# Sorting the rows of three batches by expert instead of two, in a one-core attention and mixture-of-experts kernel

## The chip, the cores and the metric

The kernel runs on one core of one Trainium2 chip. The metric is the time in microseconds (us) of one execution on the device.

## What is computed

Four batches of 512 tokens, each a row of 256 float32. Cut to its shape, the reference is:

```python
h = W_tok[x]                                                     # 4 x 512 x 256
h = h + local_attention(layernorm(h)) @ Wo + bo                  # 16 heads, windows of 128, one window back
n = layernorm(h)
gate = softmax(n @ W_gate + b_gate)                              # 8 experts
combine = top-2 weights of gate, zero elsewhere                  # 4 x 512 x 8
moe = sum over e of combine[e] * (n @ W_experts[e] + b_experts[e])
out = h + full_attention(n @ W_qkv + b_qkv) + moe
```

Each row needs only two of the eight experts.

## The kernel before

The program is written engine by engine with semaphores between them. The attention runs in eight **stages**, in the order of `STAGES` (line 55): LOCAL 0, LOCAL 1, LOCAL 2, FULL 0, LOCAL 3, FULL 1, FULL 2, FULL 3, numbered 0 to 7. A stage has 16 **slots** (a group of four heads and a block of 128 keys each), and a slot has two **half slots**, so a stage has half slots t = 0 to 31. In a slot TensorE computes transposed scores (`scores`, lines 1478 and 1484), row scores of a later head (`row_scores`, lines 1456 to 1464), of which VectorE takes the maxima (`maxima`, line 971 in a FULL stage) through two PSUM banks `SC`, and probabilities times V (`times_v`, line 1505). ScalarE takes the exponentials (lines 840 and 843). The last stage has no rows of a later stage, so its slots 10 to 15 have no row scores and no maxima.

All else is laid into the half slots by the table `PREPS` (line 60): an entry `(what, batch, first)` of stage s starts the work `what` of that batch at half slot `first` of that stage; entries with a negative `first` continue from the stage before. `prep_jobs` (line 210) says at which step which job of TensorE comes; each engine and the DMA queues run the same table. All jobs of TensorE outside the slots go through two PSUM banks `R` in turn (`claim`, line 1229: a job waits until the job two before it has been read). The kinds that matter here:

- `"full"`: layer norm, transposes into `xT_full`, q, k, v, gate logits and the choice of two experts (`gate_weights`, line 1034) of a batch's FULL stage. `"out"`: the projection after local attention.
- `"dense"`, for batches 2 and 3: every expert takes all 512 rows. 16 jobs `dx` (line 1377), one in two half slots, each two row tiles of 128 by one expert; VectorE multiplies by the weight and adds it into `h` (line 1133).
- `"route"`, `"experts"`, `"combine"`, for batches 0 and 1 (`SPARSE = 2`): the rows are sorted by expert. `count_rows` (line 1337) and the steps of lines 1073 to 1105 find each row's place. GpSimd scatters the normalised rows into `x_sorted` in DRAM (`sort_rows`, line 650, 16 indirect DMAs, one a half slot). With 16 row tiles of pairs and up to 8 tiles that are filled in part there are 24 tiles, each of one expert. A job `xs` transposes two tiles (line 1359), loaded by SyncE (line 553); a job `ex` multiplies them by their experts' weights (line 1373), gathered by GpSimd (line 666, 256 KB each); VectorE copies the result (line 1119), SyncE stores it (line 559). `combine` gathers each row's two results (line 682) and VectorE adds them into `h` (line 1147).

SyncE and GpSimd run their DMAs in program order; a wait holds whatever is behind it. On SyncE these are the q/k parts (line 491), the stacked loads for the next stage (line 505), the shift rows (line 512), the loads and stores of sorted tiles, expert weights of dense batches (line 570) and the output (line 523). Before the scatters, SyncE zeroes `x_sorted` in stage 3 (line 545).

Of the kernel before, what the change touches and what calls it, by code (L numbers as in the profile page):

```python
# [82 lines left out]
SPARSE = 2  # L83
# [179 lines left out]
def tower(nc, x, tok_w, wq, bq, wk, bk, wv, bv, wo, bo, wqkv, bqkv, wg, bg, wexp, bexp, out):  # L263
    with ExitStack() as ctx:
# [200 lines left out]
        def _(sp):  # L465
# [96 lines left out]
            def load_weights(b, e):  # L562

                n = W_BEFORE[b] + e
                if n == 0:
                    sp.wait_ge(s_qk_ps, at(STAGE[LOCAL, B - 1], 4, 4))
                    sp.wait_ge(s_v_ps, V_BEFORE[STAGE[LOCAL, B - 1] + 1])
                if n >= W_RING:
                    sp.wait_ge(s_ex_ps, last_bank(n - W_RING) + 1)
# [12 lines left out]
            for s in range(len(STAGES)):  # L582
                kind, b = STAGES[s]
                for u in range(UNITS):
# [25 lines left out]
        def _(pool):  # L610
# [49 lines left out]
            def gather_weights(j):  # L660
# [11 lines left out]
            def gather_output(n, k):  # L672
                if n == 0 and k == 0:
# [101 lines left out]
        def _(act):  # L775
# [12 lines left out]
            def copy_x(p, c):  # L788
# [777 lines left out]
```

## Time and profile before

| | us |
|---|---|
| median of 3 runs | 643.25 (642.73 to 643.69) |
| the profiled execution | 642.01 |
| its span, first to last instruction | 640.2 |
| busy: TensorE / VectorE / ScalarE / GpSimd | 561.2 / 419.1 / 296.3 / 182.7 |
| mean granted TensorE clock | 0.959 of full speed |

The profile shows one execution. Stages are told apart by their first transposed-score matmul: stage 3 begins at 225.33 us of the span, stage 4 at 295.87, stage 5 at 362.42, stage 6 at 461.61, stage 7 at 556.00. A float32 matmul stands as two records in the trace. An engine's busy share is an average over these stages.

### The profile page before, as it was taken

To read this page: it belongs to the slowest core of one execution; us is meant where nothing else is said; L and a number is where in the kernel's file an instruction comes from. 1 tells how busy PE (TensorE), PEld (TensorE's weight loads), DVE (VectorE), ACT (ScalarE), POOL (GpSimd) and SP (SyncE) were. 2 spreads that over 40 slices of the span, in tenths; PEclk is the share of its full clock that TensorE was granted. 3 is DMA by queue.
4 is the path that set the end of the run, shared out by engine and by line. 5 is a ranking of instruction groups with operands and counts; after the bars stand their busy time and mean duration, and the time that the engine had idled before them with its cause. 6 is when DMAs were issued, how large, how long until landed. Compare 5 with 4: busy or idle time off the path is not lost.

```text
span 640.2 us, 9968 instructions
## 1 busy us (share of the span) xinstructions
PE 561.2 (88%) x3455; PEld 301.9 (47%) x3455; DVE 419.1 (65%) x940; ACT 296.3 (46%) x558; POOL 182.7 (29%) x238
## 2 busy tenths in 40 slices
PE   3867699889999898998998899989998898999994
PEld 3434455555565333444543455544444454555441
DVE  7237557675867888577478777756865465678830
ACT  0312346444644575476264353535554454444452
POOL 3774216222322501022132233211143231043201
PEclk9879799999989999999797799999999899999998
DMA  6386425342344235532325134504149668232310
GB/s 171 106 171 135 128 59 173 64 94 62 109 84 83 83 104 129 132 104 79 83 49 167 43 84 124 124 9 132 50 143 253 181 171 225 68 93 73 100 51 33
DMA packets 42417, 69.23 MB, mean 108 GB/s; under 512 B 6648, under 2 KB 35968, under 8 KB 39296
## 3 DMA queue, kind: packets, MB, share of 16 engines
q1 hardware_dynamic: 38144, 56.02, 34.4%
q0 software_dynamic: 4224, 12.59, 6.7%
q8 instruction: 28, 0.46, 0.3%
q14 instruction: 21, 0.17, 0.1%
HBM read 45.25 MB, written 23.07 MB: 107 GB/s over the span
## 4 chain that ended last, share of the span: by engine, by line
PE 66%; DVE 16%; issue 6%; DMA 6%; ACT 2%; SPq 2%; POOL 1%; POOLq 0%; DVEq 0%; ACTq 0%
PE OB L1505 11%; PE R L1387 9%; PE R L1285 8%; PE SC L1456 7%; PE ST L1478 6%; PE R L1300 5%; DVE neg_max L971 4%; PE SC L1461 3%; PE R L1373 3%; DMA QS<-shiftT 2%; PE ST L1484 2%; DMA xs<-x_sorted 2%; PE R L1333 2%; PE R L1402 2%; PE SC L1464 2%
## 5 line engine op out<-in xcount | busy, mean ns | idle before, releaser
L971 DVE TENSOR_REDUCE neg_max<-SC 128x1 f32<-128x512 f32 x256 | 171.1, 686 | 93.2 <-PE SC L1456 89.2
L840 ACT ACTIVATE prob<-ST 128x512 f32<-128x512 f32 x256 | 136.8, 598 | 125.1 <-PE ST L1478 119.2
L1505 PE MATMUL OB<-prob,VS 128*32 128x512 f32 (+2 forms) x1024 | 108.3, 496 | 0.1
L1456 PE MATMUL SC<-KS,QS 96*128 96x512 bf16 x256 | 98.1, 392 | 8.7 <-DVE neg_max L971 6.5
L843 ACT ACTIVATE prob<-ST 128x512 f32<-128x512 f32 (+1 forms) x128 | 68.5, 544 | 79.8 <-PE ST L1484 79.1
L709 POOL TENSOR_SCALAR_AFFINE_SELECT prob<-prob 128x512 f32<-128x512 f32 x64 | 41.0, 640 | 154.4 <-ACT prob L843 154.3
L1478 PE MATMUL ST<-QS,KS 98*128 98x512 bf16 x256 | 78.6, 384 | 2.0 <-ACT prob L840 1.9
L979 DVE TENSOR_REDUCE neg_max<-SC 128x2 f32<-128x512 f32 x64 | 44.1, 688 | 25.7 <-PE SC L1464 25.4
L976 DVE TENSOR_REDUCE neg_max<-SC 128x1 f32<-128x128 f32 (+1 forms) x128 | 39.4, 349 | 30.1 <-PE SC L1464 30.0
L1461 PE MATMUL SC<-KS,QS 96*128 96x256 bf16 (+1 forms) x256 | 55.3, 269 | 3.8 <-DVE neg_max L976 1.9
L1484 PE MATMUL ST<-QS,KS 98*128 98x256 bf16 (+1 forms) x256 | 48.1, 271 | 9.4 <-DMA QS<-shiftT 9.4
L1464 PE MATMUL SC<-mask_q,ident_bf 128*128 128x128 bf16 x256 | 51.6, 225 | 0.0
L781 ACT ACTIVATE parts<-R,qk_bias 128x512 bf16<-128x512 f32 x32 | 22.0, 687 | 60.0 <-PE R L1285 58.4
L1456 PEld LDWEIGHTS SC<-KS,QS 96*128 96x128 bf16 x256 | 25.0, 98 | 51.2 <-DVE neg_max L971 32.8
L695 POOL TENSOR_TENSOR parts<-rest,parts 128x512 bf16<-128x512 f32 x32 | 37.3, 1168 | 40.1 <-ACT parts L786 22.4
L944 DVE SCALAR_TENSOR_TENSOR rest<-R,qk_bias,parts 128x512 f32<-128x512 f32 x32 | 23.9, 748 | 27.3 <-ACT parts L781 26.3
L719 POOL TENSOR_TENSOR h<-h,AO 128x256 f32<-128x256 f32 x16 | 11.6, 727 | 102.3 <-DVE AO L1013 74.6
L1478 PEld LDWEIGHTS ST<-QS,KS 98*128 98x128 bf16 x256 | 24.7, 98 | 32.2 <-ACT prob L840 11.2
L1461 PEld LDWEIGHTS SC<-KS,QS 96*128 96x128 bf16 x256 | 25.3, 101 | 27.9 <-DVE neg_max L976 10.2
L1505 PEld LDWEIGHTS OB<-prob,VS 128*32 128x32 f32 x1024 | 20.4, 109 | 36.7 <-issue 33.1
L1285 PE MATMUL R<-xT_full,w_qkv 128*128 128x512 f32 x64 | 33.0, 608 | 3.0 <-DVE VS L956 3.0
L1484 PEld LDWEIGHTS ST<-QS,KS 98*128 98x128 bf16 x256 | 22.7, 102 | 25.3 <-issue 17.2
(147 smaller groups left out, 807.2 us busy)
## 6 DMA issues: line engine op xcount, KB each, us to landing
scratch<-parts SPq DMA_DIRECT2D x96, 128.0 KB
QS<-scratch SPq DMA_DIRECT2D x16, 384.0 KB, 5.2
KS<-scratch SPq DMA_DIRECT2D x16, 384.0 KB, 4.9
QS<-scratch SPq DMA_DIRECT2D x16, 256.0 KB, 3.8
KS<-scratch SPq DMA_DIRECT2D x16, 256.0 KB, 4.5
x_sorted<-ys SPq DMA_DIRECT2D x24, 128.0 KB, 3.5
xs<-x_sorted SPq DMA_DIRECT2D x12, 256.0 KB
y_sorted<-ys SPq DMA_DIRECT2D x12, 256.0 KB
```

Source lines behind the costliest of these rows:

```text
L840: act.activation(prob[:, u % 2, e, :], src[:, :], ACT.Exp, scale=SCALE).then_inc(s_prob, 1)
L843: act.activation(prob_local[:, u % 2, u // 2 % 2, 2 * e:2 * e + 2, 0:w], src[:, :].rearrange("p (i w) -> p i w", i=2)[:, :, 0:w], ACT.Exp, ...
L971: dve.tensor_reduce(own_max[:, i, head:head + 1], bank[:, :], AX.X, ALU.max, negate=True).then_inc(s_max, 1)
L979: dve.tensor_reduce(own_max[:, 2:4, head], bank[:, :].rearrange("p (w k) -> p w k", w=2), AX.X, ALU.max, negate=True).then_inc(s_max, 1)
L1285: mm = pe.matmul(bank[:, :], w, xT_of(p)[:, c, :], start=(c == 0), stop=(c == NC - 1))
L1387: mm = pe.matmul(bank[:, t % 2 * D:(t % 2 + 1) * D], xT_full[b % 2][:, c, t * P:(t + 1) * P], w_exp[n % W_RING][:, c, :], start=(c == 0), ...
L1456: pe.matmul(bank[:, :], Q[0:SHIFT_ROW, head, i * P:(i + 1) * P], K[0:SHIFT_ROW, head, :], start=True, stop=True).then_inc(s_sc_ps, 1)
L1461: pe.matmul(bank[:, first:last], Q[0:SHIFT_ROW, head, w * P:(w + 1) * P], K[0:SHIFT_ROW, head, max(w - 1, 0) * P:(w + 1) * P], start=(w % ...
L1464: mm = pe.matmul(bank[:, last - P:last], ident_bf[:, :], mask_q[:, :], start=False, stop=(w % 2 == 1), skip_group_check=True)
L1478: mm = pe.matmul(bank[:, :], K[0:KROWS, g * GH + e, keys], Q[0:KROWS, g * GH + e, :], start=True, stop=True)
L1484: mm = pe.matmul(bank[:, i * 2 * P:i * 2 * P + w], K[0:KROWS, head, keys], Q[0:KROWS, head, kt * P:kt * P + w], start=(i == 0), stop=(i == 1),
L1505: mm = pe.matmul(OB[VW * i:VW * (i + 1), columns], VS[s % 3][:, kt, v:v + VW], p_of, start=(kt == 0), stop=(kt == NT - 1), skip_group_chec ...
```

## The change

Batch 2 is sorted as well: `SPARSE` is 3, so there are 24 scatters (two a half slot), 32 expert tiles and 16 jobs `xs` and `ex`; only batch 3 stays dense. `PREPS` is laid out anew, the rings of expert weights and of results get a sixth and a third buffer, `xT_full` has one buffer instead of two, and batch 3's normalised rows go into batch 0's buffer once its rows are scattered.

```diff
     3: (("out", 2, 0), ("full", 1, 9)),
-    4: (("full", 1, -23), ("full", 2, 1), ("route", 0, 28), ("dense", 2, 32)),
-    5: (("route", 0, -4), ("dense", 2, 0), ("out", 3, 0), ("full", 3, 9), ("experts", 0, 36)),
-    6: (("full", 3, -23), ("experts", 0, 4), ("dense", 3, 29)),
-    7: (("experts", 0, -28), ("dense", 3, -3), ("combine", 0, 2), ("combine", 1, 10)),
+    4: (("full", 1, -23), ("full", 2, 1), ("route", 0, 24), ("experts", 0, 56)),
+    5: (("route", 0, -8), ("out", 3, 0), ("full", 3, 9), ("experts", 0, 24)),
+    6: (("full", 3, -23), ("experts", 0, -8), ("dense", 3, 25), ("combine", 0, 29)),
+    7: (("dense", 3, -7), ("combine", 0, -3), ("combine", 1, 5), ("combine", 2, 13)),
...
-SPARSE = 2
+SPARSE = 3
...
-BLOCKS = 2 * NT * 2
+BLOCKS = PAIR_TILES
...
-SCATTER_STEP = 4
+SCATTER_STEP, SCATTERS = 4, 2
 DENSE_JOBS = 2 * E
-W_RING, X_RING, Y_RING = 5, 3, 2
+W_RING, X_RING, Y_RING = 6, 3, 3
...
-        xT_full = [sb(f"xT_full{k}", [P, NC, T]) for k in (0, 1)]
+        xT_full = sb("xT_full", [P, NC, T])
...
-            return xn_local if kind == LOCAL or b >= SPARSE else xn_full[b]
+            return xn_local if kind == LOCAL or b == 2 else xn_full[b % 3]
...
-                    for b, slot in ((2, 3), (0, 8), (1, 12)):
+                    for b, slot in ((0, 6), (1, 10), (2, 14)):
...
                     for n in range(PAIR_TILES * TOP_K):
-                        if step == SCATTER_STEP + n:
+                        if step == SCATTER_STEP + n // SCATTERS:
                             sort_rows(n)
...
-                if kind == FULL and b > 1:
-                    act.wait_ge(s_qk_ps, at(STAGE[FULL, b - 2], 4, 4))
-                    act.wait_ge(s_v_ps, V_BEFORE[STAGE[FULL, b - 2] + 1])
+                if kind == FULL and b > 0:
+                    act.wait_ge(s_qk_ps, at(STAGE[FULL, b - 1], 4, 4))
+                    act.wait_ge(s_v_ps, V_BEFORE[STAGE[FULL, b - 1] + 1])
...
+                    if (kind, b) == (FULL, 3):
+                        dve.wait_ge(s_sorted[0], 16 * NT * TOP_K)
```

How the jobs of TensorE lie in the half slots before and now, as the table gives them:

| | before | now |
|---|---|---|
| stage 4 | `route` at t = 28 | `route` at t = 24 |
| stage 5 | 16 `dx` of batch 2, t = 0 to 30 | 4 `xs`, 3 `ex`, t = 24 to 30 |
| stage 6 | 12 `xs`, 12 `ex`, t = 4 to 28; 2 `dx` | 12 `xs`, 13 `ex`, t = 0 to 24; 4 `dx` |
| stage 7 | 14 `dx`, t = 1 to 27 | 12 `dx`, t = 1 to 23 |

TensorE in slots 0 and 1 of stage 5 (`w_q` holds an expert's weights there); before:

```order
L1478 MATMUL ST<-QS,KS 128x512 x2
L1456 MATMUL SC<-KS,QS 128x512
L1505 MATMUL OB<-prob,VS 32x128 x4
L1456 MATMUL SC<-KS,QS 128x512
L1478 MATMUL ST<-QS,KS 128x512 x2
L1456 MATMUL SC<-KS,QS 128x512
L1323 MATMUL R<-ident,AO 128x128 x4
L1387 MATMUL R<-w_q,xT_full 128x256 x2
L1456 MATMUL SC<-KS,QS 128x512
L1387 MATMUL R<-w_q,xT_full 128x256 x2
L1478 MATMUL ST<-QS,KS 128x512 x2
L1456 MATMUL SC<-KS,QS 128x512
```

and now:

```order
L1477 MATMUL ST<-QS,KS 128x512 x2
L1455 MATMUL SC<-KS,QS 128x512
L1504 MATMUL OB<-prob,VS 32x128 x4
L1455 MATMUL SC<-KS,QS 128x512
L1477 MATMUL ST<-QS,KS 128x512 x2
L1455 MATMUL SC<-KS,QS 128x512
L1322 MATMUL R<-ident,AO 128x128 x4
L1455 MATMUL SC<-KS,QS 128x512
L1477 MATMUL ST<-QS,KS 128x512 x2
L1455 MATMUL SC<-KS,QS 128x512
```

The matmuls of batch 2's dense expert are gone from between the attention's; the rest stands in the same order.

SyncE at the end of stage 5 (`parts` are batch 3's q and k); before:

```order
L505 DMA KS<-scratch 32x1x4096
L505 DMA QS<-scratch 16x4096
L570 DMA w_v<-in_L_ffn_W_experts 128x2x256
L491 DMA scratch<-parts 8x16x512 x6
L505 DMA KS<-scratch 16x4096
L512 DMA QS<-shiftT 1x4x512 x2
L491 DMA scratch<-parts 8x16x512 x6
L553 DMA xs<-x_sorted 128x2x256 x2
L512 DMA QS<-shiftT 1x4x512 x2
L505 DMA QS<-scratch 48x1x4096
L553 DMA xs<-x_sorted 128x2x256
L505 DMA KS<-scratch 48x4096
```

and now:

```order
L510 DMA QS<-shiftT 1x4x512 x2
L503 DMA QS<-scratch 32x1x4096
L551 DMA xs<-x_sorted 128x2x256
L503 DMA KS<-scratch 32x1x4096
L551 DMA xs<-x_sorted 128x2x256
L503 DMA QS<-scratch 16x4096
L489 DMA scratch<-parts 8x16x512 x6
L551 DMA xs<-x_sorted 128x2x256
L503 DMA KS<-scratch 16x4096
L551 DMA xs<-x_sorted 128x2x256
L510 DMA QS<-shiftT 1x4x512 x2
L489 DMA scratch<-parts 8x16x512 x6
```

Four loads of sorted tiles (line 551 now) moved ahead, between the stacked loads and the writes of the parts; the stage's last pair of shift rows, which had none ahead of it, now has four.

GpSimd from stage 4's end through stage 5; before:

```order
L709 AFFINE_SELECT prob<-prob 128x4x128 x6
L656 DMA x_sorted<-xn_full,slots 3072x256 x11
L689 TENSOR_TENSOR var_eps<-var,eps 128x4
L691 TENSOR_TENSOR rstd<-var_eps,minus_half 128x4
L656 DMA x_sorted<-xn_full,slots 3072x256
L719 TENSOR_TENSOR h<-h,AO 128x4x64
L656 DMA x_sorted<-xn_full,slots 3072x256 x4
L719 TENSOR_TENSOR h<-h,AO 128x4x64
L695 TENSOR_TENSOR parts<-rest,parts 128x512 x4
L719 TENSOR_TENSOR h<-h,AO 128x4x64
L666 DMA w_exp<-in_L_ffn_W_experts,w_rows 128x512 x2
```

and now:

```order
L706 AFFINE_SELECT prob<-prob 128x4x128 x5
L650 DMA x_sorted<-xn_full,slots 4096x256 x4
L706 AFFINE_SELECT prob<-prob 128x4x128
L650 DMA x_sorted<-xn_full,slots 4096x256 x12
L650 DMA x_sorted<-xn_local,slots 4096x256 x8
L686 TENSOR_TENSOR var_eps<-var,eps 128x4
L688 TENSOR_TENSOR rstd<-var_eps,minus_half 128x4
L716 TENSOR_TENSOR h<-h,AO 128x4x64 x2
L692 TENSOR_TENSOR parts<-rest,parts 128x512
L663 DMA w_q<-in_L_ffn_W_experts,w_rows 128x512
L663 DMA w_k<-in_L_ffn_W_experts,w_rows 128x512
L692 TENSOR_TENSOR parts<-rest,parts 128x512
```

All 24 scatters now stand ahead of batch 3's layer norm, with one mask of local probabilities between the fourth and the fifth, and gathers of weights stand between batch 3's third parts.

## Rows read from the trace of the kernel before

**Rows 1.** The page, part 4: shares of the chain that ended last:

```profile
PE 66%; DVE 16%; issue 6%; DMA 6%; ACT 2%; SPq 2%; POOL 1%; POOLq 0%; DVEq 0%; ACTq 0%
```

**Rows 2.** Windows, stages 3 to 7: length, PE, PEld, DVE, ACT, POOL busy, clock, DMA, GB/s:

```profile
225.33:295.87 70.54, 65.98 (x392) 29.38 (x389) 51.96 (x121) 44.92 (x86) 8.13 (x9) 1.00 0.43 113
295.87:362.42 66.55, 57.19 (x391) 28.99 (x390) 47.03 (x117) 27.95 (x53) 16.66 (x23) 0.87 0.34 92
362.42:461.61 99.19, 95.11 (x488) 52.12 (x485) 70.77 (x156) 45.68 (x86) 23.67 (x25) 0.98 0.32 81
461.61:556.00 94.39, 84.03 (x457) 45.59 (x456) 56.34 (x97) 45.76 (x85) 25.71 (x28) 0.98 0.65 182
556.00:640.25 84.25, 72.90 (x385) 35.51 (x383) 48.75 (x103) 37.70 (x72) 18.76 (x21) 0.97 0.21 66
```

**Rows 3.** The page, part 5: the maxima of a FULL stage:

```profile
L971 DVE TENSOR_REDUCE neg_max<-SC 128x1 f32<-128x512 f32 x256 | 171.1, 686 | 93.2 <-PE SC L1456 89.2
```

**Rows 4.** TensorE in order of time, stage 5: start, us, instructions, idle before:

```profile
397.39 1.13 PE L1387 MATMUL R<-w_exp,xT_full 128*128 128x256 f32 x4
398.36 0.38 PE L1456 MATMUL SC<-KS,QS 96*128 96x512 bf16 x1
398.57 1.03 PE L1387 MATMUL R<-w_exp,xT_full 128*128 128x256 f32 x4
399.44 0.60 PE L1478 MATMUL ST<-QS,KS 98*128 98x512 bf16 x2
```

**Rows 5.** TensorE in order of time, stage 6:

```profile
475.94 0.63 PE L1359 MATMUL R<-ident,xs 128*128 128x128 f32 x4
476.40 1.03 PE L1373 MATMUL R<-w_exp,xsT 128*128 128x256 f32 x4
477.27 0.38 PE L1456 MATMUL SC<-KS,QS 96*128 96x512 bf16 x1
477.49 1.03 PE L1373 MATMUL R<-w_exp,xsT 128*128 128x256 f32 x4
478.35 0.60 PE L1478 MATMUL ST<-QS,KS 98*128 98x512 bf16 x2
```

**Rows 6.** Windows, stages 3 and 5: slots 0 to 9, and 10 to 15 of stage 5:

```profile
225.33:271.08 45.75, 42.47 (x237) 18.96 (x234) 33.56 (x71) 26.49 (x50) 1.95 (x3) 1.00 0.50 127
...
362.42:424.62 62.20, 60.58 (x317) 34.67 (x314) 43.25 (x96) 26.93 (x50) 17.57 (x19) 0.98 0.37 90
424.62:461.61 36.99, 34.52 (x172) 17.45 (x171) 27.52 (x60) 18.75 (x36) 6.10 (x6) 1.00 0.24 66
```

**Rows 7.** Windows, single slots: stage 6 slots 0 and 3, stage 7 slots 12 and 13 together, 14:

```profile
461.61:464.76 3.15, 3.02 (x18) 0.78 (x17) 2.54 (x4) 2.75 (x6) 0.58 (x1) 1.00 0.73 216
475.28:480.32 5.04, 5.04 (x30) 2.85 (x28) 3.15 (x5) 3.10 (x6) 0.94 (x1) 1.00 0.62 153
...
615.58:624.95 9.37, 8.73 (x47) 4.64 (x46) 2.43 (x6) 4.72 (x9) 0.00 (x0) 1.00 0.08 27
624.95:627.40 2.45, 2.13 (x14) 0.45 (x12) 0.88 (x2) 1.97 (x4) 1.20 (x2) 1.00 0.01 3
```

**Rows 8.** Waits in stage 6: who waited for whom, us in total, times, longest:

```profile
PE R L1359 <- DMA xs<-x_sorted: 6.1, 3, 2.4
...
DVE ys L1119 <- DMA y_sorted<-ys: 2.9, 2, 1.6
...
PE R L1373 <- DVE AO L1013: 2.6, 2, 1.3
```

**Rows 9.** L656, the scatters: durations ns min/median/max, starts:

```profile
L656 POOL DMA_INDIRECT x_sorted<-xn_full,slots x16: 954/959/1117, 363.9 to 405.0; - x16
```

**Rows 10.** L666, the gathers of expert weights: issue to landing:

```profile
DMA to landing us min/median/max: 3.7/4.0/7.1
```

**Rows 11.** Windows, stage 5 slot 0:

```profile
362.42:367.82 5.40, 5.40 (x29) 3.12 (x25) 3.43 (x9) 2.00 (x4) 1.78 (x2) 0.72 0.07 26
```

**Rows 12.** All in order of time, the last instruction of the engines:

```profile
633.33 0.72 POOL L719 TENSOR_TENSOR h<-h,AO 128x256 f32<-128x256 f32 x1 [4.24 <-DVE AO L1013]
```

More of the change, by code:

```diff
@@ L86 @@
 TILE_JOBS = EXPERT_TILES // 2
-BLOCKS = 2 * NT * 2
+BLOCKS = PAIR_TILES
 ROUTE_STEPS = 13
-SCATTER_STEP = 4
+SCATTER_STEP, SCATTERS = 4, 2
 DENSE_JOBS = 2 * E
-W_RING, X_RING, Y_RING = 5, 3, 2
+W_RING, X_RING, Y_RING = 6, 3, 3
 LOAD_STEP, W_STEP, DENSE_W_STEP, STORE_STEP, ADD_STEP = -4, -3, -4, 4, 6
-EX_BEFORE = {2: 0, 0: DENSE_JOBS, 3: DENSE_JOBS + TILE_JOBS}
-W_BEFORE = {2: 0, 0: E, 3: E + EXPERT_TILES}
+EX_BEFORE = {0: 0, 3: TILE_JOBS}
+W_BEFORE = {0: 0, 3: EXPERT_TILES}
 def at(b, per_batch, k):
@@ L148, in last_bank @@
 def last_bank(n):
-    if n < W_BEFORE[0]:
-        return 2 * n + 1
     if n < W_BEFORE[3]:
@@ L449, in xT_of @@
             kind, b = STAGES[p]
-            return xT_local if kind == LOCAL else xT_full[b % 2]
+            return xT_local if kind == LOCAL else xT_full
         def xn_of(p):
             kind, b = STAGES[p]
-            return xn_local if kind == LOCAL or b >= SPARSE else xn_full[b]
+            return xn_local if kind == LOCAL or b == 2 else xn_full[b % 3]
         def dense_no(b, e):
@@ L564, in load_weights @@
                 n = W_BEFORE[b] + e
[L565 to L569, printed above, removed]
+                sp.wait_ge(s_ex_ps, last_bank(n - W_RING) + 1)
                 sp.dma_start(w_exp[n % W_RING][:, :, :], wexp[e].rearrange("(c p) n -> p c n", p=P))\
@@ L604, in _ @@
                 sp.wait_ge(s_written[m], 32 * PARTS * len(STAGES))
-            for k in range(Y_RING):
-                sp.wait_ge(s_stored[k], ring_count(TILE_JOBS - Y_RING + k, Y_RING))
+            for i in range(TILE_JOBS - Y_RING, TILE_JOBS):
+                sp.wait_ge(s_stored[i % Y_RING], ring_count(i, Y_RING))
             sp.wait_ge(s_out, 16 * B)
@@ L664, in gather_weights @@
                     pool.wait_ge(s_route, 13)
-                pool.wait_ge(s_ex_ps, last_bank(n - W_RING) + 1)
+                    pool.wait_ge(s_qk_ps, at(STAGE[LOCAL, B - 1], 4, 4))
+                    pool.wait_ge(s_v_ps, V_BEFORE[STAGE[LOCAL, B - 1] + 1])
+                if n >= W_RING:
+                    pool.wait_ge(s_ex_ps, last_bank(n - W_RING) + 1)
                 pool.indirect_dma_start(
@@ L677, in gather_output @@
                     pool.wait_ge(s_xs_ps, TILE_JOBS)
-                    for j in range(Y_RING):
-                        pool.wait_ge(s_stored[j], ring_count(TILE_JOBS - Y_RING + j, Y_RING))
+                    for i in range(TILE_JOBS - Y_RING, TILE_JOBS):
+                        pool.wait_ge(s_stored[i % Y_RING], ring_count(i, Y_RING))
                 if n >= len(y) and k == 0:
@@ L1386, in dense_expert @@
                     for c in range(NC):
-                        mm = pe.matmul(bank[:, t % 2 * D:(t % 2 + 1) * D], xT_full[b % 2][:, c, t * P:(t + 1) * P],
+                        mm = pe.matmul(bank[:, t % 2 * D:(t % 2 + 1) * D], xT_full[:, c, t * P:(t + 1) * P],
                                        w_exp[n % W_RING][:, c, :], start=(c == 0), stop=(c == NC - 1))
```

## The prediction

> **What bounds the kernel now.** I read the chain of waits first, then busy time by stage, then the order of TensorE's instructions, and last what it waits for. Two thirds of the chain that ended last is TensorE, 16% VectorE [rows 1]. By stage [rows 2], TensorE is busy 95.1 of 99.19 us in stage 5, 84.0 of 94.39 in stage 6 and 72.9 of 84.25 in stage 7; VectorE 70.8, 56.3 and 48.8. So in the stages that the change touches, time that TensorE is spared is time of the kernel, until VectorE's maxima take over. The best measure of that point is stage 3: it is the same FULL attention with the same `out` and `full` work at the same half slots as stage 5, only without dense jobs, and it took 70.54 us against 99.19.
>
> **Prices.** A job `dx` takes, from its start to the next instruction, 0.97 us for its first tile and 0.87 for its second: 1.84 us [rows 4]. A job `xs` takes 0.46 us, a job `ex` 0.87 and 0.86: 1.73 us, together 2.19 [rows 5].
>
> **The change part by part, by TensorE's work.**
> - Stage 5 loses 16 `dx` (-29.4 us) and gains 4 `xs` and 3 `ex` (+1.8 and +5.2): -22.4.
> - Stage 6 gains one `ex` and two `dx`: +1.7 and +3.7 = +5.4.
> - Stage 7 loses two `dx`: -3.7.
> - The count of rows takes four more matmuls of a few columns, under 0.2 us; it comes four half slots earlier in stage 4, where TensorE idles 9 of 66.55 us [rows 2]. VectorE's choice for batch 2 adds five small instructions there. I take 0 for both, with 1 us either way.
>
> Sum: -20.7 us, within one.
>
> **The same by slots, which holds waits too.** Stage 5, slots 0 to 9, took 62.20 us with ten `dx`; the same slots of stage 3 took 45.75 [rows 6]. A FULL slot 0 with no job took 3.15 [rows 7], some 0.6 more than stage 3's, which follows a LOCAL stage; so about 46.3 now, -15.9, or 1.6 a job rather than 1.84, since part of the cover of VectorE's maxima goes. Slots 10 to 15 (36.99 us [rows 6]) lose six `dx` at 1.84 and gain 4 `xs` and 3 `ex`, -11.0 + 7.0 = -4.0. Stage 5 thus takes about 79.3, -19.9. In stage 6 a slot without a job took 3.15 us and one with `xs` and `ex` 5.04 [rows 7]: +1.9 for the pair. Its first slots fill, its last ones change `ex` for `dx`, and one of three waits for a tile's load, which come where the load was queued behind the shift rows (half slots 8, 16, 24), goes, since half slot 24 has no `xs`; another may come at the end of stage 5. The three cost 6.1 us [rows 8]. So +5.4 less about 2, +1 for the new one: +4. In stage 7 slots 12 and 13 take 9.37 us with two `dx`, and slot 14, with none, 2.45 [rows 7]; allowing 0.6 for turning one group of outputs, -3.9. Sum: -19.8. The two ways give -20.7 and -19.8; I take -20.3.
>
> **What is hidden.** Eight more scatters on GpSimd at 0.96 us [rows 9]: all 24 are issued from half slot 28 of stage 4 to 7 of stage 5, four of them ahead of the last mask of local probabilities. That is 24 x 0.96 = 23 us in 12 half slots of about 2 us, so GpSimd may fall a few us behind, and has slot 4 free before batch 3's layer norm needs it in slot 5. The first load of sorted tiles, at half slot 20, waits at the head of SyncE's queue for all of them, with stacked loads, parts and the next shift rows behind it; by then 12 half slots, over 25 us, have passed. Eight more weight gathers, issued four half slots ahead of use, land 4.0 us later at the median, 7.1 at most [rows 10]; the cover is two slots of 5 us, and TensorE waits for none before. Eight more 128 KB zero stores lie in stage 3's slots 12 to 15. Copies on ScalarE and VectorE replace adds, and VectorE's total falls. Four loads and stores more, and eight weight loads fewer, keep SyncE level. Batch 2's output now waits for its gathered rows, but from about half slot 26, two slots before the last store is issued; what stands after the last add (it starts at 633.33 [rows 12]) I leave as it is.
>
> **Sum and forecast.** The profiled execution took 642.01 us, 1.24 under the median. 642.0 - 20.3 = 621.7; against the median of 643.25, **623.0 us**, -3.1%. A difference under 0.2% could not be told from none.
>
> **Rivals.**
> - *VectorE paces the cleared slots.* With two `SC` banks a slot cannot be shorter than four maxima, 4 x 0.686 = 2.7 us [rows 3], plus hand-overs. If the twelve cleared slots of stage 5 gave back half of 20.3, the time would be 633. Against it: stage 3, with VectorE busy 52.0 of 70.54 us and the same work. For it: stage 3's last slots have cheaper rows, stage 5's do not. 0.08.
> - *TensorE's clock.* Less work may lower it. The granted clock was 1.00 in stage 3 without any `dx`, 0.87 in stage 4, which has the idle time, and 0.72 in stage 5's slot 0 [rows 2, 11], the lower level (1.2 GHz) for over half of it. If stage 5's cleared 46 us ran at stage 4's 0.87, 12 us of it would be at 1.2 GHz and up to 6 us longer: 629. The Trainium skill (TensorE: Matmul & The Clock Gate, Part 4: PE-mode transpose) says that transposes do not count as TensorE being busy; by that rule, with 16 more transposes and 52 fewer matmuls in stage 5, this rival would be the forecast, 629. Here stage 6, with the twelve `xs`, was granted 0.98 [rows 2], so the trace does not bear it out. 0.10.
> - *Deeper rings give more.* The third result buffer takes away VectorE's wait for stores (2.9 us), and shifted loads all three waits for tiles (6.1) [rows 8]; if all of both stood on the path, 642.0 - 20.3 - 7 = 614.7, or 616 against the median. 0.06.
> - *Slower: weights arrive late.* Each of 16 `ex` needs two gathered tiles of 256 KB, which now share the DMA engines with batch 3's parts and stage 6's stacked loads at the end of stage 5, where stage 6 alone had a share of 0.65 [rows 2]. It decides from a landing of 10 us on: each us beyond costs 16 us over the sixteen jobs. At 11.5 us it takes 24 and gives 647. The longest landing was 7.1 [rows 10], and none was waited for. 0.03.
> - *The change does not do what it says*, since the freed time only turns into waits, for maxima or banks `R`: about 643. 0.02. Nothing in stage 3 looks like it.
>
> **How the numbers follow.** The forecast has 0.71. Its own range is 619.5 to 626: the two sums, 1 us for stage 4, and up to 3 us for one more stretch at the lower clock. The clock rival (629) is taken in, and half of the first one's give-back: **618.0 to 629.5**. Outside lie most of VectorE's case, late weights, no effect and most of the deeper rings. Faster by over 0.2%: all but the last two, 0.95; within 0.2%: 0.02; slower: 0.03.
>
> **What would show it.** Right: stage 5 about 79 us, stage 6 about 98, stage 7 about 80, stages 0 to 4 as before; 128 fewer records of `dx` matmuls (two for each of 64), and 32 more of `ex`; VectorE's idle time before its maxima smaller in stage 5; TensorE's idle time before `xs` near 6 us. Wrong: stage 5 at 85 or more with TensorE idle before row scores (VectorE), or a clock under 0.9 there (clock); waits of TensorE before `ex` for weights; a wait of `out` or of the end for gathered rows.

## The result and the profile after

| | us |
|---|---|
| the kernel before, median of 4 runs | 643.47 (642.73 to 647.74) |
| the changed kernel, median of 4 runs | 660.09 (655.81 to 663.16) |
| ratio | 1.024, 95% interval 1.0161 to 1.0318 |
| its profiled execution | 662.04, span 660.3 |

In these runs the change made the kernel 2.4% slower; 3.1% faster was forecast. On the page of the changed kernel TensorE is busy for 559.3 us, hardly less than before (561.2), at a lower mean clock (0.926 against 0.959):

```profile
span 660.3 us, 9830 instructions
...
PE 559.3 (85%) x3379; PEld 293.5 (44%) x3379; DVE 415.3 (63%) x925; ACT 298.4 (45%) x562; POOL 207.2 (31%) x262
```

Busy time by stage of the changed kernel, stages 3 to 7 (start and end; length; busy time and count by engine; granted clock, share of the DMA engines, GB/s), against [rows 2]:

```profile
227.30:297.86 70.56, 65.99 (x392) 29.38 (x389) 51.98 (x121) 44.91 (x86) 8.13 (x9) 1.00 0.46 120
297.86:368.71 70.85, 61.13 (x395) 30.54 (x394) 50.62 (x127) 28.13 (x53) 22.15 (x29) 0.80 0.33 95
368.71:466.83 98.12, 80.91 (x401) 36.52 (x397) 58.78 (x121) 47.40 (x90) 36.71 (x39) 0.92 0.40 108
466.83:576.42 109.59, 92.85 (x481) 52.47 (x480) 58.80 (x102) 45.56 (x85) 25.69 (x28) 0.94 0.59 167
576.42:660.31 83.89, 69.43 (x369) 32.54 (x367) 50.27 (x107) 37.60 (x72) 24.68 (x26) 0.96 0.24 71
```

Stage 3 is untouched. In stage 5 TensorE's busy time fell from 95.1 to 80.9 us and VectorE's from 70.8 to 58.8, and yet the stage lasts 98.12 us, as before (99.19). Stage 6 took 15.2 us more, for 5.4 of added work by the prediction's prices (TensorE was busy 8.8 us more in it, at a clock of 0.94 against 0.98). Stage 7's TensorE time fell by 3.5 us as the prediction's step had it, its length by 0.4. What TensorE was spared has turned into waits.

Two kinds of wait are new. The table of waits of the changed kernel (engine, line and what it waited for; us in total, times, longest), four of its rows:

```profile
PE R L1358 <- DMA xs<-x_sorted: 15.3, 4, 6.4
DVE neg_max L970 <- remote: 10.2, 3, 3.7
ACT xT_local L804 <- remote: 6.7, 2, 4.1
POOL x_sorted L650 <- remote: 4.5, 2, 2.4
```

The first was 6.1 in three waits [rows 8]. "Remote" means that the semaphore moved on just before the engine did, but that no instruction which could have moved it ended within 1.5 us before. The kernel before has no such row among its largest waits. The timeline of the changed kernel in stage 5's slot 1 (start, us, engine, line, instruction, idle time before it) shows what it is:

```profile
371.79 0.39 PE L1455 MATMUL SC<-KS,QS 96*128 96x512 bf16 x1
...
372.45 0.38 PE L1455 MATMUL SC<-KS,QS 96*128 96x512 bf16 x1
...
373.31 0.96 POOL L650 DMA_INDIRECT x_sorted<-xn_full,slots  x1 [0.30 <-issue]
374.58 0.96 POOL L650 DMA_INDIRECT x_sorted<-xn_full,slots  x1 [0.31 <-issue]
375.77 0.59 ACT L823 COPY OT<-OB 128x512 f32<-128x512 f32 x1 [3.62 <-remote]
375.81 0.69 DVE L970 TENSOR_REDUCE neg_max<-SC 128x1 f32<-128x512 f32 x1 [3.57 <-remote]
...
376.55 0.10 PEld L1455 LDWEIGHTS SC<-KS,QS 96*128 96x128 bf16 x1 [3.51 <-issue]
```

The row scores were computed by 372.2. VectorE, idle, takes their maximum at 375.81; ScalarE picks up a finished output at 375.77, in the same instant; TensorE then stands still for want of a free bank. Only GpSimd goes on here, issuing one scatter every 1.27 us; at 381.77 it too has stood 2.4 us for a signal of TensorE. I call this a **late signal**: a finished matmul of which the waiting engine learns over 1 us later. The trace also keeps the times at which semaphores moved: for three matmuls that ended by 371.9, 372.2 and 372.6 that is 375.75, 375.78 and 375.81. So the engines went on as soon as the semaphores let them. Whether the last writes of the matmuls or only the news of them was late cannot be told, since the ends of matmuls are modelled. There are several late signals up to 381.5 and again near 388 to 393. The DMA engines were not full during the first ones: their share is the last but one number (0.25) in the first of these two windows of the changed kernel (from 389 to 394 it was 0.74). The second window is slot 0 of stage 6, for later.

```profile
372.00:382.60 10.60, 5.98 (x25) 2.06 (x24) 2.73 (x5) 2.87 (x7) 6.60 (x7) 0.77 0.25 87
...
466.83:479.70 12.87, 6.50 (x29) 3.69 (x28) 3.09 (x5) 3.27 (x7) 1.90 (x2) 0.73 0.68 202
```

The waits for sorted tiles stand in TensorE's timeline of the changed kernel at these four places:

```profile
443.26 1.10 PE L1358 MATMUL R<-ident,xs 128*128 128x128 f32 x4 [3.53 <-DMA xs<-x_sorted]
...
474.01 1.10 PE L1358 MATMUL R<-ident,xs 128*128 128x128 f32 x4 [6.37 <-DMA xs<-x_sorted]
...
506.03 0.71 PE L1358 MATMUL R<-ident,xs 128*128 128x128 f32 x4 [3.31 <-DMA xs<-x_sorted]
...
531.03 0.88 PE L1358 MATMUL R<-ident,xs 128*128 128x128 f32 x4 [2.13 <-DMA xs<-x_sorted]
```

They are the jobs at half slots 24 of stage 5 and 0, 8 and 16 of stage 6. SyncE's timeline there shows that the loads stand behind the shift rows (L510), and at the stage's end behind six writes of parts (L489) and a store too:

```profile
434.84 1.23 SPq L510 DMA_DIRECT2D QS<-shiftT  x2
436.51 0.60 SPq L503 DMA_DIRECT2D QS<-scratch  x1
437.23 0.50 SPq L551 DMA_DIRECT2D xs<-x_sorted  x1
...
461.84 1.32 SPq L510 DMA_DIRECT2D QS<-shiftT  x2
463.21 3.71 SPq L489 DMA_DIRECT2D scratch<-parts  x6
466.96 0.48 SPq L557 DMA_DIRECT2D y_sorted<-ys  x1
467.48 0.47 SPq L551 DMA_DIRECT2D xs<-x_sorted  x1
```

### The profile page after: what moved, and what is told of

Same layout as the page of the kernel before. It is cut to its first block, busy times and chain, and to the rows that moved or that the text cites. A ratio compares the mean times of both kernels' runs of the same rounds, so it can differ in the third digit from the quotient of the medians.

```text
span 660.3 us, 9830 instructions
## 1 busy us (share of the span) xinstructions
PE 559.3 (85%) x3379; PEld 293.5 (44%) x3379; DVE 415.3 (63%) x925; ACT 298.4 (45%) x562; POOL 207.2 (31%) x262
## 4 chain that ended last, share of the span: by engine, by line
PE 60%; DVE 19%; issue 6%; DMA 6%; ACT 3%; SPq 2%; POOL 1%; another core or an unknown queue 1%; POOLq 0%; DVEq 0%; ACTq 0%
PE OB L1504 11%; PE R L1284 9%; PE SC L1455 7%; DVE neg_max L970 6%; PE R L1299 5%; PE ST L1477 5%; PE R L1372 4%; DMA xs<-x_sorted 4%; PE R L1386 3%; PE SC L1460 3%; PE ST L1483 2%; DMA QS<-shiftT 2%; PE R L1332 2%; PE R L1401 2%; PE SC L1463 2%
## 5 line engine op out<-in xcount | busy, mean ns | idle before, releaser
L1455 PE MATMUL SC<-KS,QS 96*128 96x512 bf16 x256 | 100.7, 405 | 20.4 <-DVE neg_max L970 12.3
L1504 PE MATMUL OB<-prob,VS 128*32 128x512 f32 (+2 forms) x1024 | 110.3, 504 | 0.1
L1477 PE MATMUL ST<-QS,KS 98*128 98x512 bf16 x256 | 79.3, 386 | 2.8 <-ACT prob L837 2.0
L1477 PEld LDWEIGHTS ST<-QS,KS 98*128 98x128 bf16 x256 | 24.7, 99 | 36.3 <-ACT prob L837 13.6
L1284 PE MATMUL R<-xT_full,w_qkv 128*128 128x512 f32 x64 | 34.6, 622 | 3.6 <-DVE VS L955 3.6
L1504 PEld LDWEIGHTS OB<-prob,VS 128*32 128x32 f32 x1024 | 20.6, 110 | 35.7 <-issue 32.4
```

The lines of the kernel that those rows point to most:

```text
L1284: mm = pe.matmul(bank[:, :], w, xT_of(p)[:, c, :], start=(c == 0), stop=(c == NC - 1))
L1455: pe.matmul(bank[:, :], Q[0:SHIFT_ROW, head, i * P:(i + 1) * P], K[0:SHIFT_ROW, head, :], start=True, stop=True).then_inc(s_sc_ps, 1)
L1477: mm = pe.matmul(bank[:, :], K[0:KROWS, g * GH + e, keys], Q[0:KROWS, g * GH + e, :], start=True, stop=True)
L1504: mm = pe.matmul(OB[VW * i:VW * (i + 1), columns], VS[s % 3][:, kt, v:v + VW], p_of, start=(kt == 0), stop=(kt == NT - 1), skip_group_chec ...
```

## The experiments

My theory after this: (A) two scatters a half slot, issued back to back, hold up the signals of other engines in stage 5; (B) the loads of sorted tiles stand behind the shift rows, a queue that the new half slots made worse. The rival to A was that stage 5, cleared of its dense jobs, is paced by something else and the scatters only lie beside it; the rival to B, that the DMA engines are full in stage 6.

### One scatter a half slot (e1_one_scatter, and again e8_one_scatter_again)

```diff
-SCATTER_STEP, SCATTERS = 4, 2
+SCATTER_STEP, SCATTERS = 4, 1
```

> The changed kernel with one scatter a half slot instead of two (24 scatters, half slot 28 of stage 4 to 19 of stage 5). Burst theory: back-to-back scatters make the other engines' waits longer, so stage 5's slots 1 and 3 (10.6 and 7.7 us) fall back to under 5 us and the kernel gets 10 to 15 us faster than the change, 645 to 650. Rival (the number of scatters, or something else that the new layout does to stage 5, counts, not their rate): the lost time is only spread over more slots, and the kernel stays within 4 us of 660.

Measured: 648.43 us (644.36 to 649.82), ratio 1.0114 (1.0043 to 1.0184). One late signal, of 1.1 us, is left (below), and stage 5 takes 84.51 us in place of 98.12; stage 6 stays where it was:

```profile
364.20:448.71 84.51, 76.11 (x401) 34.97 (x398) 58.47 (x121) 46.91 (x90) 38.66 (x41) 0.97 0.48 128
448.71:558.74 110.03, 92.76 (x481) 52.53 (x480) 58.72 (x102) 45.55 (x85) 25.68 (x28) 0.94 0.60 166
```

So the rival to A is out: stage 5 can run in 84.5 us with all 24 scatters in it.

### Two scatters a half slot in the kernel before (e2_burst_before)

```diff
-                        if step == SCATTER_STEP + n:
+                        if step == SCATTER_STEP + n // 2:
```

> The kernel before with its 16 scatters issued two a half slot, in 8 half slots of stage 5. Burst theory: stage 5 gets 5 to 10 us longer (16 scatters against the change's 24), 648 to 653. Rival (rate does not count): 643, within 1 us, since GpSimd has nothing else to do there.

Measured: 644.49 us (642.25 to 650.38), ratio 1.0063 (1.002 to 1.0105). Late signals, with waits up to 3.2 us, came in slots 2 and 3 of stage 5, without anything of the change but the pairs. The stage took 100.64 us against 99.19, not the 5 to 10 us more that were expected: the dense jobs gave TensorE other work meanwhile, which may have covered most of the delay. Stage 6 took 98.41 us against 94.39, for which I have no cause.

### Loads ahead of the shift rows (e3_loads_ahead), and both (e4_both)

SyncE issues the loads of a slot's sorted tiles before that slot's shift rows, stacks and parts:

```diff
-                        if step == LOAD_STEP + 2 * i:
-                            load_sorted(i)
...
+                    for what, c, first in PREPS[s]:
+                        for i in range(TILE_JOBS):
+                            if what == "experts" and LOAD_STEP + 2 * i + first in (2 * u, 2 * u + 1):
+                                load_sorted(i)
```

> The changed kernel, with each load of sorted tiles issued by SyncE ahead of the shift rows of its slot instead of behind them (and behind the parts). Queue theory: TensorE's four waits for xs loads (3.5 us in stage 5, 11.8 in stage 6) shrink to 3 us in all, and the kernel gets 9 to 12 us faster than the change, 648 to 651. Rival (the loads are late because of the DMA engines' load, not because of their place in the queue): waits of 10 us or more stay, and the kernel gains under 3 us.

> Both edits together on the changed kernel. If both theories hold and the losses add: 634 to 640. If the waits only come to be somewhere else (one loss hides behind the other): 645 or more.

Measured: e3 640.71 us (633.32 to 645.39), ratio 0.9967 (0.9924 to 1.001); e4, which has one scatter a half slot as well, 628.40 (625.78 to 630.79), ratio 0.9791 (0.9714 to 0.9868). On that chip e1 took 648.43, so the order of SyncE's queue alone is worth 20.0 us (15.8 against e8's 644.16). Both gained more than was expected (9 to 12 us for e3, 634 to 640 us for e4). Stages 5 and 6 of e4:

```profile
367.13:447.82 80.69, 74.59 (x400) 34.43 (x397) 58.48 (x121) 46.91 (x90) 38.72 (x41) 0.99 0.52 137
447.82:543.12 95.30, 89.50 (x481) 50.49 (x480) 58.69 (x102) 45.45 (x85) 25.67 (x28) 0.98 0.68 189
```

and what is left of the waits for tiles in it:

```profile
PE R L1360 <- DMA xs<-x_sorted: 1.6, 2, 0.8
```

SyncE's rows of e4 (the line of the loads with its first and last start; the shift rows before stage 5's slot 12) show the first load issued at 414.2 us, ahead of the shift rows of 420.91, and the others moved up behind it:

```profile
L549 SPq DMA_DIRECT2D xs<-x_sorted x16: 360/514/1397, 414.2 to 500.5; - x16
```

```profile
420.91 1.57 SPq L510 DMA_DIRECT2D QS<-shiftT  x2
```

The rival to B is out: with the waits gone the DMA engines move the same bytes sooner, at a share of 0.68 in stage 6 instead of 0.59.

### The same in the kernel before (e7_before_loads_ahead)

> The kernel before with the loads of sorted tiles issued ahead of the shift rows, as in e3. The three waits for xs (6.1 us) go and nothing else changes: 636 to 638, against 642 for the kernel before. So the sorting of the third batch, both repairs made, would be worth what e4 and e5 have beyond that, 9 to 13 us. If the waits sit elsewhere then: 641 to 643.

Measured: 633.97 us (632.35 to 635.35), ratio 0.9879 (0.9838 to 0.992). Stage 6 took 87.51 us against 94.39. The kernel before had the same fault, three waits of 6.1 us together [rows 8], and lost 6.9 us of stage 6 by them; 636 to 638 us had been expected.

```profile
461.75:549.26 87.51, 82.39 (x457) 45.27 (x456) 56.28 (x97) 45.42 (x85) 25.72 (x28) 1.00 0.71 196
```

### Experts in odd half slots (e5_odd_half_slots), later expert numbers (e6_late_tile_experts)

In e4, slots 1 and 2 of stage 6 take 8.1 and 10.0 us where slot 3 takes 5.0: batch 3's projection falls into the half slots of `xs`. e5 is e4 with every job of the sorted tiles one half slot later; e6 is e5 with the table of the tiles' experts, on VectorE, four half slots later.

```diff
-    5: (("route", 0, -8), ("out", 3, 0), ("full", 3, 9), ("experts", 0, 24)),
-    6: (("full", 3, -23), ("experts", 0, -8), ("dense", 3, 25), ("combine", 0, 29)),
-    7: (("dense", 3, -7), ("combine", 0, -3), ("combine", 1, 5), ("combine", 2, 13)),
+    5: (("route", 0, -8), ("out", 3, 0), ("full", 3, 9), ("experts", 0, 25)),
+    6: (("full", 3, -23), ("experts", 0, -7), ("dense", 3, 27), ("combine", 0, 30)),
+    7: (("dense", 3, -5), ("combine", 0, -2), ("combine", 1, 6), ("combine", 2, 14)),
...
-                    if step == 3:
+                    if step == 7:
```

(The last pair of lines is e6's alone.)

> Both repairs, and the sorted tiles' jobs on odd half slots, so that no half slot has the biases' job as well as xs and ex. Crowding theory (three jobs in half slots 2 and 4 of stage 6 keep TensorE from the attention for up to 5 us, so the others go idle): slots 1 and 2 of stage 6 fall from 18.1 to 13 or 14 us, the kernel to 623 to 626. Rival (odd half slots already have the shifts and the outputs to turn, so the crowd only moves): 627 to 631.

> e5 with VectorE's five steps for the tiles' experts four half slots later (half slot 31 of stage 4 instead of 27). If these steps and the routing's other steps on VectorE, now ahead of slot 14's biases and outputs, cause stage 4's 3.5 us more (slot 14 took 8.2 us instead of 6.0): slot 14 falls to 6 to 7 us, the kernel gains 1 to 2 us on e5, 622 to 623. If it is TensorE's lower clock there, for other reasons: slot 14 within 0.5 us of 8.2.

Measured: e5 624.12 us (621.26 to 625.39), ratio 0.9722 (0.9686 to 0.9759); e6 623.47 (622.26 to 626.4), ratio 0.9728 (0.9687 to 0.9769). Both beat the kernel before. Stage 6 of e5:

```profile
446.27:538.38 92.11, 89.33 (x473) 47.74 (x472) 56.37 (x100) 44.91 (x84) 25.67 (x28) 1.00 0.68 193
```

It is 3.2 us shorter than e4's, with one `dx` moved to stage 7, which is 0.6 longer. Slots 1 and 2 took 15.3 us together, where 13 or 14 were expected: the crowd thinned, but did not go. e6 shortened stage 4 (67.36 against 70.21) and lengthened stage 5 (81.91 against 80.18): no gain that can be told. Of that lengthening 1.2 us lies in slots 1 and 8, each of which has a short late signal in e6 (below) and none in e5, and 0.4 in slot 15, after the moved steps. Against e7, the repaired kernel before, e5's ratio gives 0.9722 / 0.9879 = 0.984: sorting the third batch is worth some 10 us, once both kernels have the loads ahead (e5's odd half slots included).

### What about the scatters delays the signals (m1, m2, m3, m4, m5)

Four kernels add work for GpSimd to stage 3 of the kernel before, where nothing else moves. m1 has 24 more scatters of 128 rows, two a half slot, each to its own tensor with consecutive rows; m3 the same, one a half slot; m2 has 16 gathers in their place; m5 is m1 with the rows 24 apart in one tensor.

```diff
+                        if s == STAGE[FULL, 0]:
+                            for j in range(24):
+                                if t == j // 2:
+                                    extra(j)
```

m4 is the changed kernel with the scatters going to consecutive rows of spare tensors; it leaves out the sorting itself, the tiles hold zeros.

```diff
-                    x_sorted, bass.IndirectOffsetOnAxis(ap=slots[:, b * NT + t, k:k + 1].bitcast(U32), axis=0),
+                    x_parts[n], bass.IndirectOffsetOnAxis(ap=row_int[:, 0:1].bitcast(U32), axis=0),
```

> The kernel before with 24 more scatters (128 rows of 1 KB each, from one constant tile into spare DRAM), two a half slot in half slots 0 to 11 of stage 3, where GpSimd is idle. If back-to-back scatters by themselves hold up TensorE's signals: delays of 1 to 4 us between a row-score matmul and its maxima appear in stage 3, which has none, and stage 3 grows from 70.5 to 76 us or more. Rival (it needs what stage 5 has besides): stage 3 within 1 us. At the end, if GpSimd's DRAIN grows with the indirect DMAs issued, it takes 2.0 us longer (6.7 to 8.7).

> The kernel before with 16 more gathers (128 rows of 1 KB from the token table into free tiles), two a half slot in half slots 0 to 7 of stage 3. If it is GpSimd's back-to-back issue of indirect DMAs: the same delays as with scatters, stage 3 at 74 us or more. If it is the scatter (writes to DRAM): none, 70.5. DRAIN 1.3 us longer.

> The same 24 more scatters, one a half slot in half slots 0 to 23 of stage 3. Rate theory: no delays, stage 3 within 1 us of 70.5; DRAIN 2.0 us longer. If the number counts: stage 3 at 75 us or more here too.

> The changed kernel, whose 24 scatters go to 128 rows in a row of 24 spare tensors instead of to the rows' places in x_sorted (so the sorted tiles hold zeros). Address theory (rows strewn over the 4 MB of x_sorted hold something up): the delays of TensorE's signals in stage 5 are gone, slots 1 and 3 under 5 us, the kernel 10 us or more faster than the change. Rival (the burst does it in that place whatever the addresses): slots 1 and 3 stay at 10 and 7 us, 655 to 662.

> The kernel before with 24 more scatters, two a half slot in stage 3 as in m1, but with rows 24 rows (24 KB) apart. Address theory: delays of 1 to 4 us between row-score matmuls and maxima appear in stage 3, and it takes 78 us or more, against 75.4 for m1. Rival: as m1, no delays, 75.4.

| | us | ratio (95%) | the stage with the bursts | late signals |
|---|---|---|---|---|
| m1, pairs, consecutive | 649.93 | 1.0134 (1.0074 to 1.0194) | stage 3: 75.4 | none |
| m2, gathers | 641.21 | 0.9997 (0.9967 to 1.0028) | stage 3: 71.1 | none |
| m3, one a half slot | 643.31 | 0.9963 (0.9918 to 1.0009) | stage 3: 70.8 | none |
| m4, change, consecutive | 658.26 | 1.026 (1.0203 to 1.0318) | stage 5: 97.6 | up to 3.7 us |
| m5, pairs, strewn | 655.41 | 1.0218 (1.0151 to 1.0285) | stage 3: 80.4 | up to 5.2 us |

m1 missed: its stage 3 grew by 4.8 us, but all of it stands in slot 7 (9.2 us, 4.6 before), where the backlog of GpSimd makes the layer norm late. A plain queue effect, without late signals. m5 had late signals in a stage where m1 had none, m4 had them with consecutive rows. Addresses alone thus do not decide. But m1, m2 and m3 ran on one chip at one time and m4 and m5 on another, which counts for more than it seemed (next section). The clearest late signal of all is m5's (timeline, stage 3):

```profile
231.83 0.39 PE L1470 MATMUL SC<-KS,QS 96*128 96x512 bf16 x1 [0.33 <-issue]
...
236.76 0.69 DVE L985 TENSOR_REDUCE neg_max<-SC 128x1 f32<-128x512 f32 x1 [4.99 <-remote]
236.86 1.08 ACT L854 ACTIVATE prob<-ST 128x512 f32<-128x512 f32 x2 [5.21 <-remote]
```

### The same kernels in further sessions (m6, m7, r1, r2, e9)

A session is what stands behind one label here: the program set up on a chip, with all its executions. The expectations call it a load. m6 is m1, m7 is m5, r1 and r2 are the changed kernel, e9 is e3, e8 is e1, each unchanged. Sessions that ran on one chip at one time are a group here: the result's; e1 to e4; m1, m2, m3 and e5; m4, m5, e6 and e7; m6, m7 and r1; r2 and e8; e9.

> The kernel before with 24 extra scatters in stage 3, two a half slot, to contiguous rows, once more. If what the addresses look like decides, the profile shows again no signal of TensorE that comes late (none over 0.5 us) and stage 3 near 75 us, as in the run before it. If it is chance from one load of the program to another, stalls of 1 to 5 us show up behind row-score matmuls in stage 3, and it goes to 78 to 82 us.

> The same with all scatters to one tensor of 3072 rows, rows 24 apart, once more. If the addresses decide, stage 3 is near 80 us again with late signals up to 5 us in two slots or more. If it is chance from load to load, it may as well come out near 75 us without them.

> The changed kernel once more, for its profile. If the stalls in stage 5 belong to the program (its order and addresses), slots 1, 3, 4 are again those over 7 us and stage 5 is 98 us within 3. If they come by chance while scatters are two a half slot, stage 5 stays over 90 us but other slots carry them.

> The changed kernel once more, now timed in five rounds beside the kernel before. If the stalls of stage 5 belong to how the program was loaded or to the chip it runs on, the runs of one load agree with each other: either all near 645 us with stage 5 near 84 us, or all near 660 us with stage 5 near 98 us. If they come by chance from execution to execution, both kinds are among these runs and they spread over 15 us.

> The changed kernel with one scatter a half slot, on the same chip. If two a half slot cost by the stalls alone, it equals the changed kernel within 3 us wherever that has a stage 5 of 84 us, and is some 12 us faster where the changed kernel has a stage 5 of 98 us. If pairs of scatters cost something of their own, it is faster on every chip.

> The changed kernel with the loads of the sorted rows ahead of the shift rows, two scatters a half slot, on a further load. If it is loaded without the late signals (stage 5 near 81 us), pairs of scatters cost nothing and it stands with the version of one scatter a half slot, 626 to 631 us. If the late signals are there again (stage 5 over 90 us), it comes out at 636 to 645 us as before.

Measured: m6 651.89 us, m7 647.83, both without late signals (stage 3: 76.4 and 75.4); r1 645.21, also without, against both of its expectations. In r2 twelve executions of the changed kernel took 641.38 to 647.57, median 644.94, ratio **1.0043** (1.0014 to 1.0072); e8, on the same chip, 644.16 (642.03 to 651.25), ratio 1.0048 (1.0016 to 1.0081). e9 had late signals up to 3.8 us: 638.80 (633.56 to 641.84), ratio 0.9947 (0.992 to 0.9974). Stages 4 to 6 of r2:

```profile
292.67:362.66 69.99, 59.92 (x395) 30.29 (x394) 50.19 (x127) 28.05 (x53) 22.14 (x29) 0.82 0.33 96
362.66:447.12 84.46, 76.06 (x401) 34.99 (x397) 58.51 (x121) 47.03 (x90) 36.71 (x39) 0.97 0.46 125
447.12:556.03 108.91, 92.73 (x481) 52.19 (x480) 58.75 (x102) 45.55 (x85) 25.68 (x28) 0.94 0.58 168
```

and stages 5 and 6 of e9:

```profile
361.37:452.53 91.16, 77.37 (x400) 34.77 (x397) 58.95 (x122) 47.73 (x89) 37.16 (x39) 0.94 0.44 120
452.53:547.94 95.41, 89.29 (x481) 50.64 (x480) 58.78 (x102) 45.17 (x85) 25.68 (x28) 0.98 0.67 189
```

The same program therefore ran in two ways, at 660.09 us and at 644.94, told apart by stage 5 almost alone: 98.12 and 84.46. The executions of one session of the changed kernel agree (4 at 656 to 663, 12 at 641 to 648), so the difference is not made anew at each execution; e3's ten and e9's twelve spread more widely (633 to 645, 634 to 642), and each session has one profile. Nor is it the chip: r2 ran on the one on which m4 and m5 had late signals. e9 differs from e4, on another chip, by 10.4 us in time, 10.5 in stage 5, 0.1 in stage 6. Of eleven sessions with pairs of scatters six had late signals (the changed kernel's first, e2, e3, e9, m4, m5) and five had none (m1, m6, m7, r1, r2).

Of nine profiles without pairs six had none (before, e5, e7, e8, m2, m3). But e1, e4 and e6 had short ones, with one scatter a half slot: where GpSimd had fallen behind, four or five scatters stood back to back, about 1.3 us apart, all the same. The first two rows are of e6, slot 1 of stage 5, the last two of e1, slot 8 (e4 and e6 have the like there):

```profile
366.20 0.60 PE L1324 MATMUL R<-ident,AO 128*128 128x128 f32 x4
...
368.44 0.59 ACT L806 COPY xT_local<-R 128x512 f32<-128x512 f32 x1 [1.33 <-remote]
```

```profile
397.18 0.66 PE L1271 MATMUL R<-ident,xn_full 128*128 128x128 f32 x4
...
398.92 0.59 ACT L796 COPY xT_full<-R 128x512 f32<-128x512 f32 x1 [2.74 <-PE R L1271]
```

The semaphore of the first moved 1.6 us after its last matmul, that of the second 1.1 us, in both cases together with those of the scores beside it. They cost little: slot 1 took 4.2 us in e6 against 3.8, slot 8 5.9 in all three against 5.2 in e5 and e8, which have the same backlog.

Put by groups, the twenty profiles show something plainer. In no group did two kernels with pairs disagree: all had late signals (e2 and e3; m4 and m5) or none (m6, m7 and r1). And the short ones came only in the groups of e2 and e3 and of m4 and m5; e8, which is e1 in the group of r2, and e5, in the group of m1, have none. So whether they come seems to go with the time of the runs, whatever the program, and how long they are with how many scatters stand back to back. On one chip at one time e3, with pairs, took 640.71 us and e4, without, 628.40, so the pairs had their price there, 12.3 us. The addresses (m1 against m5) and a difference between built programs are then not needed as causes. What differs from one time to another is open, and no kernel was set up twice within a group to test it.

## Why the prediction was wrong

Forecast and measured, stage by stage, the difference against the forecast, and what it is by the runs:

| stage | forecast | measured | of that |
|---|---|---|---|
| 4 | 66.6 | 70.85 | slots 11 to 14; 2.2 of it in slot 14, routing on VectorE |
| 5 | 79.3 | 98.12 | late signals 13.7; loads behind shift rows 3.8; rest 1.4 |
| 6 | 98.4 | 109.59 | loads behind shift rows 13.6, less 2.4 |
| 7 | 80.4 | 83.89 | end of GpSimd 2.0; slots 2, 6 and 10 together 1.1; slots 12 and 13 shorter by 3.4, not 3.9 |

The 13.7 is 98.12 - 84.46 (r2), the 3.8 is 84.46 - 80.69 and the 13.6 is 108.91 - 95.30 (r2 and e4); the rest is e4 against the forecast (in stage 6, e4 lies 3.1 under it, and the first run 0.7 over r2). The stages before begin 2.0 us later than in the profile of before, which is spread between runs.

- **TensorE's work: right in stages 5 to 7.** Where neither fault stood in the way (e4), its busy time fell by 20.5 us in stage 5 (22.4 forecast), rose by 5.5 in stage 6 (5.4) and fell by 3.5 in stage 7 (3.7); stage 5 took 80.69 us (79.3 forecast by slots) and stage 6 95.30 (98.4). Over the whole kernel it fell by 15.4 us and not by 20.7, since stage 5 gave back 1.9 less and stage 4, at a clock of 0.82 against 0.87, has 2.7 more. The pair of `xs` and `ex`, priced at 1.9 us, cost that in slot 0 of stage 6, but 3.7 and 4.0 in slots 1 and 2 (8.1 and 10.0 us, 4.5 and 6.0 before); e5 took back some of it.
- **"GpSimd may fall a few us behind, and has slot 4 free": a step that failed.** I costed 24 scatters as time of GpSimd and hid them beside other work. In the session of the result, what other engines had to hear came late while they were issued, at 13.7 us. Nothing in the profile of before could have priced that, as its scatters came one a half slot; but the prediction should have bounded it as it did every unseen edit. In other sessions the term is near zero, as r2's stage 5 equals e1's (84.46 and 84.51).
- **"One of three waits goes; another may come, +1": the step that failed in every session, and the largest.** I counted three waits at half slots 8, 16 and 24 and did not carry them to the new table. The `xs` at multiples of eight are now those of half slots 24, 0, 8 and 16: four, not two or three. The one at half slot 0 stands behind parts and stores as well. And a wait cost more than its own length; that the clock falls in it and what follows is crowded is my reading: slot 0 of stage 6 took 12.9 us, with 6.50 busy at a granted clock of 0.73 (row above), against 5.0 in e4, for a wait of 6.4. The four slots are 20.6 us longer than e4's for 15.3 us of waits; e7 gained 6.9 us of stage 6 for 6.1 us of waits. I had read the cause in the rows ("the load was queued behind the shift rows") and still priced it as its present sum.
- **Stage 4, "0 for both, 1 us either way": 3.4 us too low in r2, 4.3 in the first run.** The cover was TensorE's idle time, but the routing's steps run on VectorE, and in slot 14 they now come ahead of its maxima and of the adds that free banks `R`. That slot has 2.2 us of it; in r2 slots 12 and 13, where `route` now begins, have 1.0 and 0.6, which no run took apart. Slot 14, before and now:

```profile
352.50:358.50 6.00, 4.13 (x39) 2.35 (x38) 4.77 (x11) 2.02 (x4) 1.08 (x2) 1.00 0.01 1
```

```profile
355.90:364.10 8.20, 6.15 (x35) 2.85 (x35) 6.98 (x17) 2.56 (x5) 3.62 (x5) 0.59 0.05 18
```

  VectorE is busy 6.98 us of 8.20, and the same kind of matmuls takes TensorE longer at a granted clock of 0.59, nearer the lower level, than at 1.00. e6, which moves five of the steps, cut the slot to 6.7 us; of the 2.9 us that stage 4 gained, stage 5 gave back 1.7, 1.2 of it in the two slots with short late signals.
- **"What stands after the last add I leave as it is": 2.0 us too low.** GpSimd ends with one DRAIN, and the kernel with it. Its time goes with the indirect DMAs that GpSimd issued in the whole program: 72 before, 88 in m2, 96 in the changed kernel and m3. The rows of that line in these four (before, m2, m3, changed; duration of the one instruction three times, first and last start):

```profile
L264 POOLq DRAIN  x1: 6728/6728/6728, 633.3 to 633.3; - x1
```

```profile
L264 POOLq DRAIN  x1: 8035/8035/8035, 631.3 to 631.3; - x1
```

```profile
L264 POOLq DRAIN  x1: 8690/8690/8690, 633.3 to 633.3; - x1
```

```profile
L262 POOLq DRAIN  x1: 8690/8690/8690, 651.4 to 651.4; - x1
```

  (8.690 - 6.728) / 24 = 82 ns for each, and 6.728 / 72 = 93 as a first guess from the row of before would have served.
- **The rivals.** VectorE did not pace stage 5: its idle time before the maxima there was 27.0 us before and is 24.7 in r2, 21.0 in e4. The clock did fall in stage 5, to 0.92, as a result of the late signals: without them it was 0.97 (r2), and 0.99 with the loads ahead (e4). Weights were never late: TensorE waited for none. The rival of late weights had the right sign by the wrong mechanism. The rival that the freed time only turns into waits (643 us, chance 0.02) came nearest to what happened, with waits for signals and tiles in place of those for maxima or banks `R` that it named. The rival of deeper rings named the right waits, those for tiles, and expected the change to end them; it took e4's edit to do that. The clock rival's rule from the Trainium skill (TensorE: Matmul & The Clock Gate, Part 4: PE-mode transpose), that transposes do not count as TensorE being busy, has no support here: e4's stage 5, with four `xs`, was granted 0.99 where the rival priced 0.87, and e5's stage 6, with twelve, 1.00. It is not refuted either, as twelve `xs` are about 5.5 us (12 x 0.46, an estimate) of the 89.3 that TensorE was busy there.

The forecast of 623.0 is met by e5 (624.12) and e6 (623.47), but not as forecast: some 10 us of the gain come from sorting the third batch (e5 against e7) and some 8 from the order of SyncE's queue (e7, 1.2%).

## What to carry to other kernels

When work moves to new half slots, list on paper which loads then stand behind which in each in-order queue, and price every wait anew; a wait in front of TensorE cost 1.1 to 1.35 times its length here. Before spending a freed resource on a burst (GpSimd's scatters in pairs), spread it, if the schedule allows, and see in the trace that it is spread: with one a half slot no late signal was over 1.6 us, and those that came stood behind scatters which a backlog had pushed together. And time a changed program more than once, at different times, before believing its time: one session of this kernel said 2.4% slower, another 0.4%.

## What the runs showed of the hardware

- Signals of finished matmuls reached idle VectorE, ScalarE and GpSimd 1 to 8.4 us late by the semaphores' times (8.4 in m4), several at once, at or just after a run of indirect scatters of GpSimd 1.27 us apart; the DMA engines had a share of 0.25 at first, 0.74 at the last. Waits up to 5.2 us came of it. It came in six of eleven sessions with pairs of scatters, and 1.1 to 1.6 us long in three of nine others (e1, e4, e6), all in groups where kernels with pairs had it too. Sixteen gathers in pairs did not bring it, but in a group (m1 to m3) where pairs of scatters did not either, so scatters and gathers cannot be told apart. The mechanism is open; whether fewer outstanding scatters would avoid it was not tried.
- A DRAIN of GpSimd at the end costs about 82 ns for each indirect DMA issued before it: 6.73 us at 72, 8.03 at 88, 8.69 at 96.
- Where waits went, the granted clock rose: stage 6 had 0.94 with the loads behind the shift rows, 0.98 with them ahead, 1.00 in e5, at 89.3 to 92.9 us of busy time.
